# Two cross-attention layers on one core: the values multiplied in 64-row form into two banks, and small units placed in the ring of the maxima

## What is computed

```python
# layer 1; scale_vector in the reference is 1 for every key, so it changes nothing
q = (x @ Wq).reshape(B, Sq, 20, 16).transpose(0, 2, 1, 3)
k = (context @ Wk).reshape(B, Skv, 20, 16).transpose(0, 2, 1, 3)
v = (context @ Wv).reshape(B, Skv, 20, 16).transpose(0, 2, 1, 3)
scores = einsum('bhqd,bhkd->bhqk', q, k) / sqrt(16)
probs = softmax(scores, axis=-1)
out = einsum('bhqk,bhkd->bhqd', probs, v).transpose(0, 2, 1, 3).reshape(B, Sq, 320)
return out @ Wo + bo + x
```

## Time and profile before

| | us |
|---|---|
| median of three runs | 378.79 |
| lowest and highest | 377.38, 379.87 |
| the profiled execution | 379.04 |
| its span, from first to last instruction | 377.2 |
| mean granted TensorE clock in it | 0.941 |

### The profile page before, as it was taken

The page is one execution under the profiler, slowest core; times in us unless marked ns, Lnnn a source line. Parts: engine busy times, 40 slices in busy tenths (PEclk is TensorE's granted clock), DMA queues, the critical chain, the costliest instruction groups (busy, mean ns, idle before and its releaser), DMA issues.

```text
span 377.2 us, 5805 instructions
## 1 busy us (share of the span) xinstructions
PE 339.3 (90%) x1970; PEld 169.0 (45%) x1970; DVE 262.1 (69%) x474; ACT 234.3 (62%) x477; POOL 56.1 (15%) x76
## 2 busy tenths in 40 slices
PE   6797998989996999999999999989899999989976
PEld 6275676666762434443333333333334444322226
DVE  0427476566997688888799999899898999700023
ACT  2315445443333677778688787878887777886531
POOL 5043356460000000000000000000400000000000
PEclk9689999999997799999999999999999999996568
DMA  8940016149892006205554080703303600000002
GB/s 217 280 140 0 0 59 137 60 158 187 195 233 107 2 1 131 43 3 98 86 96 61 12 118 3 112 17 68 62 1 71 92 20 19 0 3 0 1 0 72
DMA packets 17509, 27.92 MB, mean 74 GB/s; under 512 B 2839, under 2 KB 9719, under 8 KB 17479
## 3 DMA queue, kind: packets, MB, share of 16 engines
q1 hardware_dynamic: 15495, 25.78, 32.6%
q10 hardware_dynamic: 1984, 1.76, 1.8%
HBM read 18.19 MB, written 9.18 MB: 73 GB/s over the span
## 4 chain that ended last, share of the span: by engine, by line
PE 67%; ACT 14%; DVE 11%; issue 4%; ACTq 2%; POOL 1%; DMA 1%; SPq 0%; DVEq 0%; POOLq 0%
PE ps L1163 21%; PE ps L881 16%; PE ps L1152 13%; PE ps L1141 10%; ACT probs L608 9%; DVE mx L778 6%; DVE parts L770 1%; PE ps L1075 1%; PE ps L974 1%; PE ps L1067 1%; PE ps L994 1%; DMA QS<-mT 1%; PE ps L1012 0%; ACTq L280 0%; ACTq L279 0%
## 5 line engine op out<-in xcount | busy, mean ns | idle before, releaser
L778 DVE TENSOR_REDUCE mx<-ps 128x1 f32<-128x512 f32 x320 | 199.5, 681 | 24.6 <-PE ps L1141 23.7
L608 ACT ACTIVATE probs<-ps 128x512 f32<-128x512 f32 x320 | 166.9, 603 | 58.1 <-PE ps L1152 57.9
L1152 PE MATMUL ps<-QS,KS 50*128 50x512 f32 x320 | 119.7, 472 | 15.2 <-ACT probs L608 12.9
L1141 PE MATMUL ps<-KS,QS 48*128 48x512 f32 x320 | 112.9, 455 | 1.5 <-DVE mx L778 1.4
L1163 PE MATMUL ps<-probs,VS 128*32 128x512 f32 x640 | 91.1, 644 | 0.0
L1141 PEld LDWEIGHTS ps<-KS,QS 48*128 48x128 f32 x320 | 51.3, 189 | 67.0 <-DVE mx L778 54.7
L1152 PEld LDWEIGHTS ps<-QS,KS 50*128 50x128 f32 x320 | 52.7, 194 | 55.9 <-ACT probs L608 43.0
L593 ACT CAST parts<-ps 128x512 fp32r<-128x512 f32 (+1 forms) x18 | 10.5, 582 | 25.9 <-PE ps L881 25.9
L1163 PEld LDWEIGHTS ps<-probs,VS 128*32 128x32 f32 x640 | 13.1, 111 | 21.6 <-ACT probs L608 17.8
L494 POOL TENSOR_TENSOR attn<-o_turned,o_rec 128x256 f32<-128x256 f32 x9 | 5.6, 621 | 109.3 <-DVE o_rec L793 109.2
L488 POOL TENSOR_TENSOR neg_p<-neg,neg_p 128x16 f32<-128x16 f32 x10 | 2.3, 232 | 117.8 <-DVE neg L789 117.8
(11 more groups left out here) (143 smaller groups left out, 394.3 us busy)
## 6 DMA issues: line engine op xcount, KB each, us to landing
KS<-k_parts SPq DMA_DIRECT2D x60, 128.0 KB, 4.5
k_parts<-parts SPq DMA_DIRECT2D x8, 512.0 KB, 2.8
QS<-q_parts SPq DMA_DIRECT2D x60, 64.0 KB, 5.3
q_parts<-parts SPq DMA_DIRECT2D x4, 512.0 KB, 4.2
xs<-in_x_dram SPq DMA_DIRECT2D x2, 640.0 KB, 8.7
out_dram<-xs SPq DMA_DIRECT2D x8, 160.0 KB, 1.8
k_parts<-parts SPq DMA_DIRECT2D x4, 256.0 KB, 3.3
cs<-in_ctx_dram ACTq DMA_DIRECT2D x1, 768.0 KB, 11.5
```

Source lines behind the costliest of these rows:

```text
L608: act.activation(probs[:, t % 2 * GH + h, :], ps[:, bank_of["s", m], :], ACT.Exp, scale=float(D1) ** -0.5).then_inc(exp_done, 1)
L778: dve.tensor_reduce(mx[:, g % BUF, at:at + 1], ps[:, bank_of["m", n], :], AX.X, ALU.max).then_inc(max_done, 1)
L1141: pe.matmul(ps[:, bank, :], QS[rows, g % BUF, pair, qt * P:(qt + 1) * P], KS[rows, g % BUF, pair, half * 512:half * 512 + 512], start=True ...
L1152: pe.matmul(ps[:, bank, :], KS[rows, g % BUF, h // 2, kt * P:(kt + 1) * P], QS[rows, g % BUF, h // 2, :], start=True, stop=True).then_inc( ...
```

## The change

The four matmuls of a step's values become eight: the first four contract over keys 0 to 63 of the tile into bank 6, the other four over keys 64 to 127 into bank 7. After a group ScalarE copies bank 6 to `o_raw` as before, and VectorE then adds bank 7 to it (`add_second_half`). The turn of a group waits for that addition. The add of a group stands ahead of the first maxima of the next group's first step in VectorE's program. As bank 7 is taken, the small units take the next bank in the ring of the maxima instead, between the third and the fourth maxima matmul. The last group's turn goes to bank 4.

```diff
@@ place_all
                 if h == 3 and t in X_AT:
-                    placed(X_AT[t], 7)
+                    placed(X_AT[t], next(m_ring))
                 if n < NM:
                     placed(("m", n), next(m_ring))
                 if m < GH * STEPS:
                     placed(("s", m), 3 + m % 3)
             if t % NKT == 0:
                 placed(("pv", t // NKT), 6)
-        placed(("turn", NG - 1), 7)
+                placed(("pv2", t // NKT), 7)
+        placed(("turn", NG - 1), 4)
@@ vector
+            def add_second_half(g):
+
+                dve.wait_ge(o_copied, g + 1)
+                dve.tensor_tensor(o_raw[:, :], ps[:, bank_of["pv2", g], :], o_raw[:, :], ALU.add).then_inc(o_added, 1)
+
...
             for t in range(STEPS):
                 g, kt = t // NKT, t % NKT
+                if kt == 0 and g > 0:
+                    add_second_half(g - 1)
                 for n in range(LEAD + 4 * t, min(LEAD + 4 * t + 4, NM)):
                     maximum(n)
...
             g, o = NG - 1, ps[:, bank_of["turn", NG - 1], :]
+            add_second_half(g)
             dve.wait_ge(o_norm, g)
@@ tensor
                 elif kind == "pv":
                     pe.wait_ge(o_copied, u[1] + 1)
+                elif kind == "pv2":
+                    pe.wait_ge(o_added, u[1] + 1)
...
             def turn_o(g):
 
-                pe.wait_ge(o_copied, g + 1)
+                pe.wait_ge(o_added, g + 1)
...
                 if kt == 0:
                     pe.wait_ge(v_staged, g + 1)
                     free_bank(("pv", g))
-                for h in range(GH):
-                    m = pe.matmul(ps[2 * D1 * h:2 * D1 * (h + 1), bank_of["pv", g], :], VS[:, g % 2, kt, h, :],
-                                  probs[:, t % 2 * GH + h, :], start=(kt == 0), stop=(kt == NKT - 1))
+                    free_bank(("pv2", g))
+                for kind, rows in (("pv", slice(0, HALF)), ("pv2", slice(HALF, P))):
+                    for h in range(GH):
+                        m = pe.matmul(ps[2 * D1 * h:2 * D1 * (h + 1), bank_of[kind, g], :], VS[rows, g % 2, kt, h, :],
+                                      probs[rows, t % 2 * GH + h, :], start=(kt == 0), stop=(kt == NKT - 1))
                 m.then_inc(pv_mm, 1)
```

More of the change, by code:

```diff
@@ L248, in two_layer_cross_attention @@
         s_mm, exp_done, pv_mm = sem("s_mm"), sem("exp_done"), sem("pv_mm")
+        o_added = sem("o_added")
         o_copied, oT_mm, turned_copied, o_rec_done, o_norm = (sem("o_copied"), sem("oT_mm"), sem("turned_copied"), sem("o_rec_done"),
```

## The result

The changed kernel took 397.94 us (median of 4 runs, 395.42 to 407.76) where the kernel before took 379.33 (4 runs, 377.38 to 380.20). The ratio is 1.048, with a 95% interval of 1.040 to 1.056. The change made the kernel slower, by 18.6 us between the medians. The profiled execution took 396.86 us, with a span of 395.0.

What follows compares the result with a forecast made beforehand. Bound: a serial ring through TensorE and one maximum, 2.70 us a plain step. Form 2.2, turns 9.8, negated maxima 2.8, projections 2.9, final matmuls and transposes 4.4, addition-only waits 1.5 add 23.6 us: 402 us, range 387 to 420.

Steps and rivals of the forecast that it cites:

- What bounds the kernel: Plain steps: a serial ring through TensorE and one maximum sets 2.70 us; VectorE's maxima alone would allow 2.41.
- The 64-row form: Values matmuls: no change-of-form cost saved, four more first passes cost 0.03 us a step, 2.2 us in all.
- The addition: VectorE's ten adds, each ahead of a group's first maxima: that first maximum starts 0.84 us later.
- The ring of three: Small units in the maxima's three banks wait for the first maximum, the fourth maxima matmul for the second, 0.60 us later.
- parts 2 and 3: The added VectorE additions and the small units in the three-bank ring: together 20.6 us up to step 74.
- turn with addition: Eight turn steps that have maxima: the fourth maxima matmul starts 1.23 us later, 9.8 us in all.
- The wait behind a unit: Next step's second maxima matmul waits for the unit's bank to be evacuated: nothing, with up to 0.1 us a step above.
- The sum: Whole kernel: 2.2 + 9.8 + 2.8 + 2.9 + 4.4 + 1.5 = 23.6 us added.
- Columns alone costing nothing: Values beside scores: 0.30 us comes off each step, plain steps meet VectorE's 2.41, 378 us in all; chance 0.14.
- Row halves queueing: Upper four values matmuls start 0.46 us late behind the lower four, 0.43 a step, some 437 us; chance 0.08.
- The clock falling more often: Two more half-clock stretches of 5.5 us as TensorE stands in turn steps: 413 us, from 408 to 420; chance 0.10.
- Partly absorbed delays: Only half of the addition's and the small units' delays count, as where ScalarE is late anyway: 391 us; chance 0.08.

Runs made afterwards that it cites:

- ring of four: The kernel before with bank 7 added to the ring of the maxima and small units taking turns in it: 377.25 us, ratio 1.009.
- rows undone: The changed kernel with full-height values matmuls over 128 rows, key tiles going to banks 6 and 7 in turn: 396.01 us, ratio 1.049.
- ring only: The kernel before with small units taking turns in the three-bank ring of the maxima and nothing else changed: 389.45 us, ratio 1.033.
- 128 × 128 form: The changed kernel with one values matmul of 128 rows by 128 columns, head 0's probabilities only, banks in turn: 405.39 us, one run.

## Why the prediction was right

The forecast was slower, 402 us in a range of 387 to 420, and 397.94 came. The mechanism was right part by part. How near the total came was in part luck, since a stretch of half clock at the end of the profiled execution of before is missing in that of the changed kernel.

- **What bounds the kernel** held: the plain step is set by the ring through TensorE and one maximum. Taking the change of form out of TensorE's part brought it to 2.42 and VectorE's floor; taking only the wait for the maximum out (ring of four) brought 0.06.
- **The 64-row form**: taken as 0 saved and 0.03 a step lost. Measured 1.9 us in 74 steps, by undoing it alone. The choice between 0.30 saved and nothing, which rested on one row of weight loads in the first layer, was right. The 0.30 itself was too small for the price of changing forms: without a change of form 0.31 came off a plain step before VectorE bound it, and 0.52 off the steps without maxima before ScalarE did.
- **The addition**: 0.84 forecast between the old and the new start of the first maximum behind it. Counted from the values of the step before, that start moved by 0.89 in the changed kernel and by 0.83 with the rows undone, and turn steps of the latter are 0.83 longer than with the ring only. The addition lasts 0.69.
- **The ring of three**: 13.9 us measured for it alone, and 7.0 for the addition, 20.9 together; parts 2 and 3 of the prediction have 20.6 up to step 74. (The 13.3 that were expected of the ring only were worked out with the changed kernel's steps at hand.) By kind (forecast, measured in the changed kernel): turn with addition 1.23, 1.33; negated maxima 0.35, 0.39; value projections 0.39, 0.40 in steps 3, 10 and 12; final transposes 0.48, 0.51; final matmuls 0.63, 0.57 in three of four; step 72 0.73, 0.78. The turn was short by 0.10: ScalarE's copy came 0.06 later after its values (1.19 instead of 1.13), and the turn began 0.15 after the maximum's end, where I had 0.05 for a semaphore. It now has a wait for the addition and one for the bank. The wait behind a unit, taken as nothing, was nothing behind a turn (plain steps of 2.72), but not behind the query projection: step 21 grew by 0.66, because its second maxima matmul stands for VectorE's evacuation of the projection's bank:

```profile
197.41 0.50 PE L1153 MATMUL ps<-KS,QS 48*128 48x512 f32 x2 [0.19 <-DVE parts L772]
```

- **The sum** for steps 0 to 74 was 22.7 (23.6 less what falls behind step 74), and 24.3 was measured; some 1.5 of that are steps 1 and 2, in a stretch of half clock that was 13.7 us long instead of 10.2.
- **What the sum did not have** is the clock at the end. I weighed only that it could fall more often. In the profiled execution it did not fall, where before it had. From the values of step 74 to the end before took 34.4 us, of which four steps at 4.07; the changed kernel took 27.9, with steps of 2.62. 24.3 − 6.5 is the 17.8 between the spans. At equal mean clock (before 371.1 at 0.967, the change 396.9 at 0.965) the difference is about 26 us, above the forecast; between medians it is 18.6, below it. A forecast from one profile takes over that profile's clock.
- **The rivals.** Columns alone costing nothing: refuted, plain steps are 2.72 to 2.73. Row halves queueing: the first passes of all eight matmuls begin within 0.05 us, before any second one. The clock falling more often: the reverse in the profile, though one of the four runs took 407.76. Partly absorbed delays: in one step only, step 7 with a value projection, which took 3.80 after 3.77; elsewhere the parts add up step by step.

**What stays open**: why the clock kept full at the end of the loop in the profiled executions of the changed kernel, of the ring only and of the rows undone, whose last steps do nearly the same work as those of before. One execution of each kernel is profiled, and the others differ from it in their mean clock (0.924 to 0.965 for the changed kernel, 0.943 to 0.964 for the ring only), so this may be a difference between executions and not between kernels. The 64-row form is ruled out as the only cause, since two kernels without it kept it too. The 128 × 128 form lost it again, with steps of 4.20. Busy shares don't tell them apart: TensorE was recorded busy for 82% (20.1 of 24.6 us) in the changed kernel's last steps at full clock, and for 86% in the 11.1 us ahead of the fall in the kernel before (windows of before, then after):

```profile
331.50:342.60 11.10, 9.54 (x53) 3.14 (x53) 0.25 (x1) 9.57 (x19) 0.62 (x1) 1.00 0.01 3
...
352.90:377.50 24.60, 20.13 (x185) 6.35 (x184) 0.94 (x2) 19.73 (x40) 0.62 (x1) 1.00 0.01 2
```

## What to carry to other kernels

If the cost of changing the array's form is to go, the whole difference must go: compare rows and columns of both neighbours, and look in the trace whether the next weights load while the last matmul streams. Before a small unit is put into a ring of banks, ask whose evacuation its bank waits for and who is next to want it; in a ring shorter than the step one more tenant moves each wait to the next reduction, 0.60 us later, of which 0.35 to 0.6 us a unit were left here after the slack. An addition in front of such a chain costs its own length and the wait for what it adds to. And read the steps, not the total: here the total hid 6 us of clock that no run ties to the change.

## What the runs showed that was not expected

- Full clock or not at the end of the loop goes with 6 to 9 us in this kernel, between executions of one program: 371.1 and 379 to 380 us at mean clocks of 0.967 and 0.94, and 6.5 us between the ends of the two profiles. That is more than most edits bring.
- Matmuls whose results nobody reads, placed in the idle row half, cost nothing in time (steps of 2.61 with them, 2.60 without), and the mean clock of all twelve executions with them was 0.959 to 0.972.
- Steps of 2.31 us, below VectorE's four times 0.60, occur where the form is not changed: VectorE works through ten maxima without a gap and catches up in the longer steps between. A floor from one engine bounds the mean of several steps, not each.
- With all changes of form gone the bound passed on twice: to VectorE in plain steps (2.42 us) and to ScalarE in the last steps (2.10 us). What a form costs is read where no other engine takes over.
